# Weights and tables of seven later phases loaded once during the heads and kept in SBUF, and local attention with its queries scaled on GpSimd

## What is computed

```python
x = _layernorm(x + _L0_attn_ref(x, ...))   # 16 heads of 8, full softmax attention
x = _layernorm(x + _L0_ffn_ref(x, ...))    # itself two layers of local attention + gated feed-forward
x = _layernorm(x + _L1_attn_ref(x, ...))   # 16 heads, Taylor softmax, rotary positions
x = _layernorm(x + _L1_ffn_ref(x, ...))    # silu(gate) * up, int32 weights
```

```python
h = shift_token(x); q, k, v = split(h @ wqkv)             # 8 heads of 64
q = l2norm(q) * qs; k = l2norm(k) * ksc; q, k = rotary_xpos(q, k)
sim = where(mask, -max, 8 * q @ k.T)                      # window of 64 keys back
x = x + softmax(sim) @ v @ wo
```

## Time and profile before

| | us |
|---|---|
| median of 3 runs | 2095.55 (2095.2 to 2096.95) |
| the profiled execution, its own time | 2095.52 |
| its span in the trace | 2093.5 |
| busy in the span: PE, DVE, ACT, POOL | 1681.3, 1676.9, 1169.1, 697.4 |
| heads, first to last instruction | 53.2 to 777.6 |
| local attention, first layer and second | 824.9 to 1170.8 and 1262.8 to 1611.3 |
| last feed-forward | 2003.6 to 2090.2 |

### The profile page before, as it was taken

One profiled execution on the slowest core, in us unless ns is written; L12 is line 12 of the kernel. 1 busy time (PEld: TensorE's weight loads), 2 busy tenths in 40 slices (PEclk: granted clock), 3 DMA queues, 4 the chain that ended last, 5 costly groups with the idle time before them and its releaser, 6 DMA issues. The chain is left out here.

```text
span 2093.5 us, 47784 instructions
## 1 busy us (share of the span) xinstructions
PE 1681.3 (80%) x15985; PEld 891.1 (43%) x15985; DVE 1676.9 (80%) x3448; ACT 1169.1 (56%) x2316; POOL 697.4 (33%) x531
## 2 busy tenths in 40 slices
PE   5799999999999983788888595888885752676768
PEld 3123322323232323455555362655554432565645
DVE  6799999999999916799999464999995778677546
ACT  4078878877888871577777322777775210332411
POOL 3000000000000003788888224888884333223101
PEclk9589999999999996999999897999998975887879
DMA  5200000000010004000000222000001231010022
GB/s 167 62 8 26 17 18 22 27 18 17 20 29 2 2 16 126 16 20 20 22 19 17 56 81 68 21 20 22 19 19 42 77 87 30 2 30 21 22 73 70
DMA packets 144154, 75.92 MB, mean 36 GB/s; under 512 B 53186, under 2 KB 138876, under 8 KB 143740
## 3 DMA queue, kind: packets, MB, share of 16 engines
q1 hardware_dynamic: 133444, 69.13, 11.8%
q10 hardware_dynamic: 10552, 4.70, 0.9%
HBM read 52.54 MB, written 20.98 MB: 35 GB/s over the span
## 5 line engine op out<-in xcount | busy, mean ns | idle before, releaser
L554 DVE TENSOR_REDUCE hd_top<-hd_pX 128x1 f32<-128x512 f32 x1024 | 620.2, 677 | 26.5 <-PE hd_pX L433 26.2
L537 ACT ACTIVATE hd_E<-hd_pS 128x1024 f32<-128x1024 f32 x512 | 524.3, 1024 | 194.5 <-PE hd_pS L448 177.6
L433 PE MATMUL hd_pX<-l_K,l_Q 48*128 48x512 bf16 x1024 | 353.9, 403 | 23.1 <-DMA l_Q<-q_parts 21.6
L465 PE MATMUL hd_pO<-hd_E,l_V 128*32 128x256 f32 x4096 | 330.7, 395 | 16.5 <-ACT hd_O L530 16.3
L448 PE MATMUL hd_pS<-l_Q,l_K 50*128 50x512 bf16 x1024 | 317.6, 387 | 8.7 <-issue 6.5
L1026 ACT ACTIVATE w_E<-w_pS,w_nb,w_inv_q 128x128 f32<-128x128 f32 x512 | 227.9, 459 | 38.0 <-DVE w_nb L1170 38.0
L1089 POOL TENSOR_TENSOR w_inv<-w_ss,w_mhalf 128x16 f32<-128x16 f32 x64 | 186.2, 2910 | 118.1 <-DVE w_ss L1150 118.1
L417 POOL COPY l_V<-l_v_all 128x256 f32 x12 | 4.8, 400 | 557.0 <-PE hd_pO L465 557.0
L465 PEld LDWEIGHTS hd_pO<-hd_E,l_V 128*32 128x32 f32 x4096 | 82.1, 108 | 170.5 <-issue 107.6
L448 PEld LDWEIGHTS hd_pS<-l_Q,l_K 50*128 50x128 bf16 x1024 | 61.6, 94 | 206.0 <-issue 199.0
L433 PEld LDWEIGHTS hd_pX<-l_K,l_Q 48*128 48x128 bf16 x1024 | 89.3, 94 | 125.3 <-DVE hd_top L554 97.5
(11 more groups left out here) (205 smaller groups left out, 3281.9 us busy)
## 6 DMA issues: line engine op xcount, KB each, us to landing
l_Q<-q_parts SPq DMA_DIRECT2D x192, 32.0 KB
l_K<-k_parts SPq DMA_DIRECT2D x180, 32.0 KB
m<-w_Y SPq DMA_DIRECT2D x64, 64.0 KB, 1.6
f_H<-m SPq DMA_DIRECT2D x32, 128.0 KB
f_X<-m SPq DMA_DIRECT2D x16, 256.0 KB, 3.0
q_parts<-pj_ptq SPq DMA_DIRECT2D x8, 384.0 KB
k_parts<-pj_ptk SPq DMA_DIRECT2D x8, 384.0 KB, 2.5
pj_X<-in_L_attn_embedding_dram SPq DMA_DIRECT2D x8, 256.0 KB, 3.4
```

The costliest lines, as they stand in the source:

```text
L433: nc.tensor.matmul(pX[slot][:, :], Q[m.j][rows, m.z, b, t * P:(t + 1) * P], K[m.j][rows, b, k * 512:(k + 1) * 512], start=True, stop=True) ...
L465: last = nc.tensor.matmul(pO[VW * b:VW * b + VW, cols], V[n.j][:, b * NT + g, :], E[g % SLOTS][:, b, cols], start=(g == 0 and half == 0), ...
L537: nc.scalar.activation(E[g % SLOTS][:, 2 * k:2 * k + 2, :], pS[k][:, :, :], ACT.Exp).then_inc(exped[k], 1)
L554: nc.vector.tensor_reduce(top2[m.z][:, ROW_ORDER[q], k:k + 1], pX[slot][:, :], AX.X, ALU.max).then_inc(topped, 1)
```

## The change

A new class `Kept` holds every weight and table past the heads in SBUF for the whole program. ACT issues all its loads in the heads, behind the twelve of the first K: the identity and 53 more (about 7.1 MB by the shapes). POOL then waits for all of them and prepares them once (tables times scales, mask and identity to bf16, integer weights to float32). The phases lose their own loads, waits and preparations, and SP loses the identity at the start of the heads. `Kept` has three semaphores, cleared by a scope of its own at the very end.

```diff
+class Kept:
+    LOADS = 5 + 2 * (5 + 14) + 7 + 3
...
+    def load(self, eng, a):
...
+        eng.dma_start(self.ident[:, :], a["ident"]).then_inc(self.ident_in, 16)
+        bring(self.wo0[:, :], a["L0_attn_Wo"])
...
+        for layer in range(2):
+            k = self.local[layer]
+            bring(k["wqkv"][:, :], a["L0_ffn_wqkv"][layer])
...
+            bring(k["tab"][:, :, :, :], a["rotary"])
...
+    def prepare(self, pool):
+        pool.wait_ge(self.ident_in, 16)
+        pool.wait_ge(self.arrived, 16 * self.LOADS)
...
+        nc.gpsimd.tensor_copy(self.mask[:, :, :], self.mask32[:, :, :]).then_inc(self.ready, 1)
...
+        nc.gpsimd.tensor_copy(self.cast[:, :, :], self.raw[:, :, :]).then_inc(self.ready, 1)
+        pool.wait_ge(self.ready, 15)
... phase_l0_heads
                 load(sp, 0, 0, Q, q_parts, 0)
-                sp.dma_start(ident[:, :], ident_d).then_inc(ident_in, 16)
...
                     nc.gpsimd.tensor_copy(V[h][:, :, 0:HD], v_all[:, :, h * HD:h * HD + HD]).then_inc(v_ready[h], 1)
+                kept.prepare(pool)
...
                 load(act, 0, 0, K, k_parts, 1)
+                kept.load(act, a)
... phase_window_attention, SP
-                for dst, src in ((ident[:, :], ident_d), (wqkv[:, :], w_qkv)):
-                    sp.dma_start(dst, src).then_inc(weights_in, 16)
                 for k in range(RING):
                     load_h(Tile(None, k))
... PE
-                    run(t, (turn_e, -1, 0), (score, 0), (qk, 2), (turn_e, -1, 1), (v, 1), (weigh, -1), (turn_c, 1), (project, -1), (turn, 3))
+                    run(t, (score, 0), (qk, 2), (turn_e, -1, 1), (turn_e, -1, 0), (v, 1), (weigh, -1), (turn_c, 1), (project, -1), (turn, 3))
... ACT
-                        last = nc.scalar.activation(E[:, r, p, :], pS[t.u][:, r, p, :], ACT.Exp, bias=nb[:, t.u, i:i + 1],
-                                                    scale=inv_q[:, t.u, h:h + 1], accum_out=tot[:, i:i + 1])
+                        last = nc.scalar.activation(pS[t.u][:, r, p, :], pS[t.u][:, r, p, :], ACT.Exp, bias=nb[:, t.u, i:i + 1],
+                                                    accum_out=tot[:, i:i + 1])
...
-                    nc.scalar.copy(OT[:, :, :], pO[:, :, :]).then_inc(ot_ready, 1)
+                def keep_low(t):
...
+                    nc.scalar.copy(VA[0:WINDOW, t.u, :], V[0:WINDOW, t.u, :]).then_inc(v_low, 1)
+                def keep_high(t):
...
+                        nc.scalar.copy(VA[WINDOW:P, 1 - t.u, :], V[WINDOW:P, t.u, :]).then_inc(v_high, 1)
...
-                    run(t, (take_q, 1), (take_h, 3), (exp, 0, 1), (take_et, 0, 0), (square, 3), (take_et, 0, 1), (exp, 1, 0), (take_o, 0),
-                        (take_v, 2))
+                    run(t, (take_et, -1, 0), (exp, 0, 0), (take_v, 1), (take_q, 1), (take_h, 3), (exp, 0, 1), (keep_low, 0), (keep_high, 0),
+                        (square, 3), (take_et, 0, 1))
... POOL
+                    nc.gpsimd.tensor_tensor(C[:, t.u, :, :], C[:, t.u, :, :], N[:, t.u, :, :], ALU.add).then_inc(added, 1)
...
+                    nc.gpsimd.tensor_tensor(c, c, over_heads(inv[:, :]), ALU.mult).then_inc(rotated, 1)
...
-                    run(t, (add_q, 1), (root, 2), (keep_v, 0), (keep_inv_q, 2), (add_k, 2), (scale_k, 2))
+                    run(t, (root, 2), (add, 2), (scale, 2))
... DVE
+                    nc.vector.tensor_reduce(nb[:, t.u, :], pS[t.u][:, :, :, :].rearrange("p r a t -> p (r a) t"), AX.X, ALU.max, negate=True)\
...
-                    nc.vector.tensor_tensor(e, e, rec[:, sl].rearrange("p (h a) -> p h a", a=1).broadcast_to([P, PAIRS, P]), ALU.mult)\
+                    nc.vector.tensor_tensor(E[:, r, :, :], pS[t.u][:, r, :, :], rec[:, sl].rearrange("p (h a) -> p h a", a=1).broadcast_to([P, PAIRS, P]), ALU.mult)\
...
-                    run(t, (scale_e, -1, 0), (take_k, 0), (spin_q, 1), (scale_e, -1, 1), (take_v_low, 0), (add_x, -2), (bias, 0),
-                        (sum_squares, 2), (spin_k, 2), (clamp, 2))
+                    run(t, (take_o, -2), (clamp, 1), (take_k, 0), (spin, 1, 0), (scale_e, -1, 0), (scale_e, -1, 1), (add_x, -2), (bias, 0),
+                        (sum_squares, 2), (spin, 2, 1))
```

More of the change, by code:

```diff
@@ L31 @@
 BANDS = len(PART_PAIRS) * HD
+WH = 8
+WD = 64
+INNER = WH * WD
+WINDOW = 64
+KEYS = WINDOW + P
+PAIRS = WH // 2
+HALF = WH // 2
+HIDDEN = 341
+HW = HD + 1
+SQ2 = HD * HD
+PW = 2 * SQ2
 MAX_ROWS = 2
@@ L753, in _, with phase_window_attention @@
                     st.end()
[L757 to L766, removed]
+def phase_window_attention(nc, tag, kept, layer, x_pad, x_out_d):
     NT = S // P
@@ L775, in phase_window_attention @@
         s = Scope(nc, ctx, tag)
-        ident = s.sb("ident", [P, P])
-        ident16 = s.sb("ident16", [P, P], BF16)
+        ident, ident16, mask = kept.ident, kept.ident16, kept.mask
+        wqkv, wo, tab = (kept.local[layer][n] for n in ("wqkv", "wo", "tab"))
         mhalf = s.sb("mhalf", [P, 2 * WH])
[L779 to L784, removed]
         Hs = s.sb("H", [P, RING, D])
@@ L1080, in scale_k, with scale @@
+                def scale(t):
                     pool.wait_ge(inv_ready, t.k + 1)
[L1081 to L1083 removed]
+                    pool.wait_ge(added, t.k + 1)
+                    c = heads(C[:, t.u, :, :].rearrange("p z c -> p (z c)"))
+                    nc.gpsimd.tensor_tensor(c, c, over_heads(inv[:, :]), ALU.mult).then_inc(rotated, 1)
@@ L1208, in phase_ffn @@
         s = Scope(nc, ctx, tag)
-        ident = s.sb("ident", [P, P])
+        ident = kept.ident
         mhalf = s.sb("mhalf", [P, CT])
-        wg = s.sb("wg", [P, hidden])
-        wu = s.sb("wu", [P, hidden])
-        wd = s.sb("wd", [P, KT, D])
+        W = weights(s)
+        wg, wu, wd, own, b2r = (W.kept[n] for n in ("wg", "wu", "wd", "own", "b2r"))
         Hs = s.sb("H", [P, 2, CT, D])
@@ L1246, in phase_ffn @@
         with nc.Block() as block:
-            W = weights.place(nc, s, dict(ident=ident, wg=wg, wu=wu, wd=wd, own=own, b2r=b2r, ident_d=ident_d, ready=weights_ready,
-                                          turned=weights_turned, pG=pG, width=width))
+            W.place(nc, s, dict(pG=pG))
             def reach(eng, sem, count):
@@ L1292, in _ @@
                 load_h(0, 0)
-                W.load(sp)
                 load_h(1, 1)
@@ L1509, in load @@
[L1509 to L1524 removed]
+        self.nc, self.pG = nc, k["pG"]
@@ L1546, in phase_l1_attention @@
+            last.then_inc(self.turned, 1)
+        pe.wait_ge(self.ready, 3)
+def phase_l1_attention(nc, tag, kept, x_d, theta, rope_d, x_out_d):
     NT = S // P
@@ L1833, in _ @@
                     act.dma_start(dst, src).then_inc(angles_in, 16)
-                for dst, src in ((gain[:, :], column_of(ln_w)), (bias[:, :], column_of(ln_b)), (mask1[:, :, :], mask1_d), (mask2[:, :], mask2_d)):
-                    act.dma_start(dst, src).then_inc(weights_in, 16)
-                act.wait_ge(weights_in, WEIGHTS)
                 act.wait_ge(set_up, 5)
```

327 lines of the change are left out of this document (124 added, 203 removed).

## The result

The changed kernel takes 2016.28 us, median of 4 runs (2013.7 to 2020.0), against 2096.25 us for the kernel before (2095.2 to 2101.09, 4 runs): ratio 0.9616, 95% interval 0.9593 to 0.9638. The forecast was 2015. The profiled execution took 2017.86 us by its own time, with a span of 2015.8 (before: 2095.52 and 2093.5), so its account must come to -77.7.

What follows compares the result with a forecast made beforehand. DVE was taken to set the local-attention tile's pace, in a loop with ACT. Tiles -59.4, starts -4.2, -7.0, -7.0, -6.1, heads -0.4 and +2, end +1.5 sum to -80.6 us, giving 2015; range 1985 to 2050.

Steps and rivals of the forecast that it cites:

- The period, -59.4: Local attention, both layers: tile period falls from 9.89 us by 0.99 over 60 periods, gaining 59.4 us.
- DVE 8.1: Local attention: DVE's own work per tile falls from 9.26 to 8.1 us.
- PE is the bound at 8.9: Local attention: PE's unchanged work of 8.9 us a tile becomes the period, bounds 8.5 and 9.4.
- that case: Rival, local attention: PE's own work is nearer 8.5 us a tile, 24 us less, 1991; chance 0.12.
- The reading it began with: Local attention before: DVE's small product takes 0.97 us where POOL is adding beside it, 0.17 otherwise.
- POOL: Local attention: POOL's two wide instructions take 4.6 us, upper figure 4.8; its tile 7.9 us.
- the first rival: Local attention: the path through POOL takes DVE's place; wide two at 5.6 give period 9.4, time 2045; chance 0.17.
- POOL becomes the bound, slower: Rival, local attention: wide instructions at 1.5 times the doubled cost, period 10.7, time 2125; chance 0.04.
- Starts: Phase starts: first projection -4.2 us, each local attention -7.0, last feed-forward -6.1, from earlier first loads.
- The end of the span: Program end: one more scope to clear costs +1.5 us.
- The heads' start: Heads: one issue less -0.4 us, slower issues beside 7.1 MB of loads +2, bounds 0 and +13.

Runs made afterwards that it cites:

- with E in SBUF: Changed kernel with exponentials written to SBUF and E divided in place there; 2092.5 us, ratio 0.9976 to the kernel before.
- the ring shortened: Changed kernel with ACT squaring queries and keys separately, each as soon as its matmul is done; 1991.25 us, ratio 0.9483 to the kernel before.
- the loads and tables alone: Changed kernel with the local attention's tile as before, less its loads and table work; 2072.96 us, ratio 0.9881 to the kernel before.
- one more instruction on POOL's path: Changed kernel with an extra 512-element POOL addition between each tile's wide addition and wide scaling; 2029.74 us, ratio 0.9669 to the kernel before.
- division from PSUM in the kernel before: Kernel before with exponentials written over the scores in PSUM and DVE dividing from there into E; 2068.72 us, ratio 0.986.

## Why the prediction was right, point by point

- **The period, -59.4.** The sum of the two layers' tiles was 29.1 + 30.7 = 59.8. That they agree so well is luck: two slips met. The gain of a period is 0.94 and not 0.99, and 60 x 0.94 is 56.4; the two layers gave what 64 tiles would, 64 x 0.94 = 60.
- **DVE 8.1, and why.** The value is right, and the division's way through PSUM is the part without which the rest fails: with E in SBUF the period is 10.27, slower than before.
- **PE is the bound at 8.9.** The number held by luck, and the reason did not. PE's own work is 8.5; that case stood among the rivals at 0.12, with a time of 1991. PE's rows had shown waits of 0.42 and 0.56 us and I took 9.89 less these for its work. The same instructions in another order are not the same work either: PE is busy 8.8 us a tile before and 8.53 now, and 0.17 of that is E's transposes, all eight in a row now (27.9 us in 23 tiles before, 24.1 now). What held the period at 8.94 was ACT's square and its copies in a ring with PE, which the forecast never priced, as it took ACT's 7.9 us for a load and asked only whether it was under PE's. With the ring shortened, the kernel took 1991.25.
- **The reading it began with.** Beside the product of 0.97 POOL was scaling the keys, not adding. Nothing hangs on it: the product was held either way, and it is gone.
- **POOL.** 2.36 + 1.90 = 4.26 us against 4.6 taken and 4.8 as the upper figure. The path that the first rival goes by exists and, as far as the one added instruction shows, had 0.7 us to spare in two tiles; had the two wide instructions cost 5 us or more, it would have decided.
- **POOL becomes the bound, slower.** Its argument against was the deciding one, and both halves are shown: no DVE instruction with two SBUF inputs was left, and bringing one back costs 76 us. Even then POOL idles 2.7 us a tile; it is DVE that is held.
- **Starts.** First projection -4.3 for -4.2, last feed-forward -6.9 for -6.1, local attention -6.8 and -5.9 for -7.0 each. PE's start itself moved by 8.1 in the first layer, as the load landed after 2.3 us and not 3.4; 1.4 and 1.1 us were lost again as the pipeline filled. The end of the span, with one more scope to clear, is +0.8 for +1.5.
- **The heads' start, the term that was mis-sized:** +4.9 for +1.6. I priced SP's issues, and they cost 0.7. The term that was not in the sum is the landing of the stores of maxima: 3.8 us from the first issue to PE's first scores before (101.59 to 105.40), 7.4 in the changed kernel (102.30 to 109.67), so 3.6 more. The last of the kept loads had landed at 109.2, when POOL began to prepare them. The maxima for that store were ready at 86.6, so the first Q, 1.6 us later, costs nothing by itself. These 4.3 us make up all but 0.6 of the 4.9. PE's clock looks like the rest, by the windows of the kernel before, then of the changed one:

```profile
114.00:116.00 2.00, 2.00 (x22) 0.49 (x20) 1.50 (x3) 1.15 (x2) 0.00 (x0) 0.69 0.01 2
```
```profile
114.00:116.00 2.00, 2.00 (x14) 0.42 (x13) 1.74 (x5) 0.95 (x2) 2.00 (x3) 0.50 0.00 0
120.00:122.00 2.00, 2.00 (x16) 0.33 (x12) 1.29 (x2) 1.02 (x1) 1.89 (x3) 0.53 0.00 0
```

It rises from the 1.2 to the 2.4 GHz level in the slice at 114 us before, and only at the end of the one at 120 in the changed kernel; with the loads and tables alone it rose at 116 to 118, and the heads ended 2.1 us sooner than in the changed kernel though the first scores came only 0.4 sooner. But the other runs do not bear this out. With one more instruction on POOL's path the clock came up in the slice at 120 too:

```profile
118.00:120.00 2.00, 2.00 (x16) 0.34 (x12) 1.31 (x3) 1.10 (x2) 2.00 (x3) 0.50 0.02 3
120.00:122.00 2.00, 2.00 (x20) 0.46 (x16) 1.32 (x3) 1.21 (x2) 2.00 (x5) 0.84 0.01 1
```

Yet there the first scores to the end of the heads took 673.0 us, against 673.7 in the kernel before and 674.4 in the changed one. Over the ten profiles it is 672.7 to 674.5, so 0.6 us is within what single executions differ by, and its cause stays open.

## What to carry to other kernels

Before an instruction on GpSimd is made wider, look at which DVE instructions run beside it and where their inputs lie: the time that one DVE instruction can be held is the length of one GpSimd instruction, so the wider one is only safe once the instructions of DVE that run beside it read PSUM. When one engine's work goes, do not take the next engine's busy time for the new period; follow the ring of waits once around with the durations in hand, and let a consumer start on the first half of what it waits for. Loads for later phases are free only where nothing small and urgent lands beside them: issue them behind the last transfer that somebody waits for.

## What the runs showed that was not expected

- One exponential of 128x128 lasts, by its output and by whether it has a scale operand per partition: SBUF and scale 457 ns (before), PSUM and scale 435 (division from PSUM in the kernel before), SBUF without scale 371 (E back in SBUF), PSUM without scale 344 (changed). The scale operand is worth 86 to 91 ns and PSUM 22 to 27. "ScalarE: Activation LUTs" of the Trainium skill, section "Step-by-step: what each stage is for", says that ACT is faster into PSUM than into SBUF: the trace agrees for the length of one instruction, with these small numbers, and not for the pace. From the start of one exponential to the start of the next it is 0.44 us with the scale operand and 0.35 without it, into SBUF as into PSUM. So it is the scaling of the queries on POOL that gave ACT 0.7 us a tile, about what its copies of V cost it over the copy that left (0.62 each).
- A DVE copy with a single SBUF input (1.41 us for 0.41) is held by GpSimd as a product with two inputs is.
- The root on GpSimd, 2.9 us for 16 elements, holds nothing up here: beside it the division with two SBUF inputs took 0.69 us, the same as from PSUM.
